# Last layer of a two-layer decoder: the product of attention weights and values taken for two sequences in one matmul, its two PSUM banks split by halves of the heads, and normalised once for every two units

## The chip, the core and the metric

The kernel runs on one core of one Trainium2 chip. The metric is device time in microseconds (us) of one execution. Five engines run their own instruction streams and meet only through semaphores: TensorE (PE, with its weight loads shown apart as PEld), VectorE (DVE), ScalarE (ACT), GpSimd (POOL) and SyncE (SP, which here only issues DMAs).

## The reference, cut to what matters

The program is a decoder of two layers over 32 sequences of 64 tokens with 256 channels. The change lies in the second layer's attention, a differential attention with 16 heads, each with two sub-heads of 8 channels (queries q1, q2 and keys k1, k2) and 16 channels of values that both sub-heads share. `attn1` and `attn2` are causal softmax attention of the two sub-heads over the same 16 value channels.

```python
attn1 = causal_attn_pair(q1, k1, v1, v2, mask, scale)   # softmax(q1 k1^T) [v1 v2]
attn2 = causal_attn_pair(q2, k2, v1, v2, mask, scale)
lambda_full = lambda_1 - lambda_2 + LAMBDA_INIT
f1, f2 = rfft(attn1, axis=1), rfft(attn2, axis=1)       # over the 64 tokens
attn_freq = (f1 - lambda_full * f2) * filt
attn = irfft(attn_freq, n=tgt_len, axis=1)
attn = attn * rsqrt(mean(attn * attn, -1) + EPS) * rms_weight * (1 - LAMBDA_INIT)
return attn.reshape(bsz, tgt_len, H * 2 * D) @ Wout
```

After it the layer adds a summary of a context, normalises, and multiplies by a ternary weight matrix. All of that runs in the same stage as the attention, for other blocks.

## The kernel before, in words

The last layer (`layer1` in the code) works on 8 blocks of 256 tokens (4 sequences). In a block, c = 0, 1 counts chunks of 128 tokens, which are two sequences (s = 0, 1) of 64 tokens side by side on the 128 partitions. A block has 8 units u: chunk c = u // 4, half of the heads m = u // 2 % 2, and quarter hf = u % 2. A unit holds 8 sub-heads, that is 4 heads.

What a unit goes through, each engine one or more slots after the other:

- POOL `keys` spreads the keys over a block-diagonal tile (`k_bd`, L1860).
- PE `score` multiplies queries with `k_bd` and adds the mask (L1973, L1975).
- DVE `row_max` takes the row maximum (L2277) and its negative (L2278).
- ACT `exps` takes 8 exponentials with their row sums `rs` (L2094).
- PE `turn_exp` transposes the exponentials (L1983), and DVE (even units, L2284) or ACT (odd units, L2152) copies them into `et`. `et` has the two sub-heads times the 64 keys of a sequence on its partitions, and for each head 128 columns: the 64 query tokens of sequence 0, then those of sequence 1.
- PE `pv` multiplies `et` with the values `v_bd` (L2000). `v_bd` is block diagonal over the two sub-heads, 32 columns for each head and sequence. For every head there are two matmuls, one for each sequence: 64 columns of `et` as weights, 32 columns of values streamed, written to the 64 rows of that sequence in bank `p_o[c]`. One bank thus holds all 32 sub-heads of a chunk.

After the four units of a chunk, DVE `scale(b, c)` takes the reciprocal of the 32 row sums (L2289), multiplies those of the second sub-heads by minus lambda (L2290), multiplies the bank by them (L2293) and adds the two sub-heads (L2298) into `d`. PE `mix` then applies the filter over the tokens as a matrix (L2009), ACT and DVE take the RMS norm (`rms`, L2138, L2304 to L2311, the power -1/2 on POOL at L1868, `rms_end` at L2315 and L2318), PE transposes (L1940) and multiplies by Wout (L2023), and DVE `wout` adds the residual (L2323).

The order is written out by hand. Every engine runs `for t in range(-1, NBLK + 3)` and in it slots `u in range(8)`. In slot u of pass t the unit is g = 8t + u. PE issues in a slot: `turn_exp(g-1)`, `pv(g-3)`, `score(g+2)`, and then the extras of the slot (u=0 `wout(t-2)` and `t1(t+1)`, u=1 `val(t+1)`, u=2 to 5 `qk(t+1, u-2)`, u=3 `mix(t-1)`, u=4 and 5 the last matmuls of block t-3, u=7 `attn_t(t-1)`). DVE issues `copy_exp(g-2)` for even g, then `wout(t-2)` in slot 1, then `scale(t-1, 1)` in slot 3 and `scale(t, 0)` in slot 7 (behind `rms_end(t-1)`), then `row_max(g+1)`, then `rope_qk(t+1, u-3)` in slots 3 to 6 (two products L2251, four sums L2268), then statistics, `x_apply` and others. Each engine keeps this order strictly: an instruction that waits holds all behind it.

ACT `val` writes `v_bd` for the next block but one (L2130), after the last `pv` that read the same buffer.

Of the kernel before, what the change touches and what calls it, by code (L numbers as in the profile page):

```python
# [9 lines left out]
BATCH, SEQ, DIM = 32, 64, 256  # L10
P = 128
# [3 lines left out]
TC = TOK // P  # L15
# [30 lines left out]
H1, D1 = 16, 8  # L46
SUB = 2 * H1
USUB = 8
NUNIT = SUB // USUB * TC
# [29 lines left out]
def wait(eng, sem, count):  # L79

    if isinstance(count, int) and count <= 0:
        return
    eng.wait_ge(sem, count)


def memory(nc, st):
# [6 lines left out]
    def place(at, *tensors):  # L93

        for name, shape, *dt in tensors:
# [61 lines left out]
                ("rope", [P, 2, TOK]), ("zn", [P, TC, DIM]), ("hi_q", [P, TC, DIM]), ("xa", [P, TC, DIM]),  # L157
                ("xq", [P, TC, DIM], bf16), ("xq_t", [P, KC, TOK], bf16), ("k_bd", [P, 2, USUB, SEQ]),
                ("ex", [P, 2, USUB, SEQ]), ("et", [P, 2, 4 * P]), ("k_st", [P, 2, 4, TC, SEQ]),
                ("yg", [P, 2, TC, DIM]), ("v_bd", [P, 2, TC, 2, H1, 32]),  # L160
                ("osc", [P, TC, SUB * 16]), ("d", [P, TC, DIM]), ("sq", [P, TC * DIM]))
    assert end <= Q0
    end = place(N0, ("sum_w0", [P, KC, DIM]), ("sum_w1", [P, KC, DIM]), ("wq_a", [P, KC, DIM]),
# [1528 lines left out]
def layer1(nc, T, sem, A, E, ctx_sum, ctx_total, summary, x_sh, yt, w_in, b_in, w_out, b_out, w_qk, w_v,  # L1692
# [5 lines left out]
    ALU, ACT, AX = mybir.AluOpType, mybir.ActivationFunctionType, mybir.AxisListType  # L1698
# [26 lines left out]
    S = {n: sem("z_" + n) for n in names}  # L1725
# [20 lines left out]
    def blocks(*b):  # L1746
        return all(0 <= n < NBLK for n in b)
# [181 lines left out]
    def tensor(pe):  # L1929
# [58 lines left out]
        def pv(g):  # L1988
            b, u = g // NUNIT, g % NUNIT
            c, m, hf = UT[u]  # L1990
            pe.wait_ge(S[f"e_read{g % 2}"], g // 2 + 1)
            if u == 0:
                pe.wait_ge(S["a_read"], PA["val", b] + 1)
            if u % 4 == 0:
                wait(pe, S["os_ready"], 2 * (b - 1) + c + 1)
            for q in range(4):
                h = 4 * (2 * m + hf) + q
                for s in range(2):
                    rows = slice(SEQ * s, SEQ * s + SEQ)
                    mm = nc.tensor.matmul(p_o[c][rows, h * 32:h * 32 + 32],  # L2000
                                          et[:, g % 2, q * P + SEQ * s:q * P + SEQ * s + SEQ],
                                          v_bd[:, b % 2, c, s, h, :], start=True, stop=True)
            mm.then_inc(S["pv_done"], 1)

        def mix(b):
            pe.wait_ge(S["d_ready"], 2 * (b + 1))
            done = tenant("b", "circ", b)
            for c in range(TC):
                mm = nc.tensor.matmul(p_b[:, c * DIM:c * DIM + DIM], circ[:, :], d[:, c, :],  # L2009
                                      start=True, stop=True)  # L2010
            mm.then_inc(done, 1)
# [72 lines left out]
    def scalar(act):  # L2084
        def exps(g):
            b, u = g // NUNIT, g % NUNIT
            c, m, hf = UT[u]
            act.wait_ge(S["mx_ready"], g + 1)
            wait(act, S["e_done"], g - 1)
            if u % 4 == 0:  # L2090
                wait(act, S["os_ready"], 2 * (b - 2) + c + 1)
            for j in range(USUB):
                at = USUB * (2 * m + hf) + j
                ins = nc.scalar.activation(ex[:, g % 2, j, :], p_s[g % 2][:, j * SEQ:j * SEQ + SEQ], ACT.Exp,  # L2094
                                           bias=nmx[:, g % 2, j:j + 1], scale=SCALE1,
                                           accum_out=rs[:, b % 2, c, at:at + 1])
            ins.then_inc(S["p_exp"], 1)

        def apply(n, b, src, dst, ready):
            act.wait_ge(RSTD[n][0], RSTD[n][1] + b + 1)  # L2100
            for c in range(TC):
                ins = nc.scalar.activation(dst[:, c, :], src[:, c, :], ACT.Identity,
                                           bias=nbias[:, n, c:c + 1], scale=nrs[:, n, c:c + 1])
            ins.then_inc(S[ready], 1)

        def norm1(b):
            wait(act, S["a_done"], PA["t1", b - 1] + 1 if b else 0)
            apply(1, b, x3[:, b % NX3], n1, "n1_ready")

        def norm_z(b):  # L2110
            wait(act, S["y_sum"], b)
            apply(2, b, x4[:, b % 2], zn, "z_norm")

        def norm_y(b):
            apply(3, b, zn, zn, "y_norm")

        def t1(b):
            act.wait_ge(S["a_done"], PA["t1", b] + 1)
            nc.scalar.activation(xt1[:, :, :].rearrange("p a b -> p (a b)"), p_a[:, :], ACT.Copy
                                 ).then_inc(S["a_read"], 1)  # L2120

        def val(b):

            act.wait_ge(S["a_done"], PA["val", b] + 1)
            wait(act, S["pv_done"], NUNIT * (b - 1))
            act.wait_ge(A["s_set"], A_SET + 4)
            pm = p_a[:, :].rearrange("p (c h e) -> p c h e", c=TC, e=16)
            for s in range(2):
                for o in range(2):
                    ins = nc.scalar.activation(  # L2130
                        v_bd[SEQ * o:SEQ * o + SEQ, b % 2, :, s, :, 16 * o:16 * o + 16],
                        pm[SEQ * s:SEQ * s + SEQ, :, :, :], ACT.Copy)
            ins.then_inc(S["a_read"], 1)

        def rms(b):
            act.wait_ge(S["b_done"], PB["circ", b] + 1)
            wait(act, S["ss_ready"], b)
            nc.scalar.activation(sq[:, :], p_b[:, :], ACT.Abs, scale=RMS_SCALE).then_inc(S["abs_done"], 1)  # L2138
            wait(act, S["b_done"], PB["at", b - 1] + 1 if b else 0)
            nc.scalar.activation(att[:, :, :].rearrange("p a b -> p (a b)"), p_b[:, :], ACT.Copy  # L2140
                                 ).then_inc(S["b_read"], 1)

        def at_copy(b):
            act.wait_ge(S["b_done"], PB["at", b] + 1)
            wait(act, S["b_done"], PB["wout", b - 1] + 1 if b else 0)
            nc.scalar.activation(att_t[:, :, :].rearrange("p a b -> p (a b)"), p_b[:, :], ACT.Copy
                                 ).then_inc(S["b_read"], 1)

        def copy_exp(g):
            act.wait_ge(S["e_done"], g + 1)  # L2150
            wait(act, S["pv_done"], g - 1)
            nc.scalar.activation(et[:, g % 2, :], p_e[g % 2][:, :], ACT.Copy).then_inc(S["e_read1"], 1)  # L2152

        for t in range(-1, NBLK + 3):
            for u in range(NUNIT):
                g = NUNIT * t + u
                if units(g):
                    exps(g)
                if units(g - 2) and g % 2:
                    copy_exp(g - 2)  # L2160
                if u == 0 and blocks(t - 2):
                    at_copy(t - 2)
                if u == 0 and blocks(t + 1):
                    norm1(t + 1)
                if u == 1 and blocks(t + 1):
                    t1(t + 1)
                if u == 2 and blocks(t + 1):
                    val(t + 1)
                if u == 3 and blocks(t - 2):
                    norm_z(t - 2)  # L2170
                if u == 4 and blocks(t - 1):
                    rms(t - 1)
                if u == 6 and blocks(t - 2):
                    norm_y(t - 2)
# [44 lines left out]
    def vector(dve):  # L2219
# [63 lines left out]
            wait(dve, S["pv_done"], g - 1)  # L2283
            nc.vector.tensor_copy(et[:, g % 2, :], p_e[g % 2][:, :]).then_inc(S["e_read0"], 1)  # L2284

        def scale(b, c):

            dve.wait_ge(S["pv_done"], NUNIT * b + 4 * c + 4)
            ch(nc.vector.reciprocal(rin[:, c, :], rs[:, b % 2, c, :]))  # L2289
            ch(nc.vector.tensor_scalar(rin[:, c, 1:SUB:2], rin[:, c, 1:SUB:2], neg_lam[:, 0:1], None,  # L2290
                                       ALU.mult))
            o4 = osc[:, c, :].rearrange("p (h e) -> p h e", e=16)
            nc.vector.tensor_tensor(o4, p_o[c][:, :].rearrange("p (h e) -> p h e", e=16),  # L2293
                                    rin[:, c, :].unsqueeze(2).broadcast_to([P, SUB, 16]), ALU.mult
                                    ).then_inc(S["os_ready"], 1)
            dve.wait_ge(S["os_ready"], 2 * b + c + 1)
            wait(dve, S["b_done"], PB["circ", b - 1] + 1 if b else 0)
            nc.vector.tensor_tensor(d[:, c, :].rearrange("p (h e) -> p h e", e=16),  # L2298
                                    o4[:, 0:SUB:2, :], o4[:, 1:SUB:2, :], ALU.add
                                    ).then_inc(S["d_ready"], 1)  # L2300

        def rms(b):
# [65 lines left out]
        for t in range(-1, NBLK + 3):  # L2368
            for u in range(NUNIT):
# [2 lines left out]
                    copy_exp(g - 2)  # L2372
                if u == 1 and blocks(t - 2):
                    wout(t - 2)
                if u == 3 and blocks(t - 1):
                    scale(t - 1, 1)
                if u == 7 and blocks(t - 1):
                    rms_end(t - 1)
                if u == 7 and blocks(t):
                    scale(t, 0)  # L2380
                if units(g + 1):
                    row_max(g + 1)
                if 3 <= u < 7 and blocks(t + 1):
# [175 lines left out]
```

## Time and profile before

| | us |
|---|---|
| median of 3 runs | 1423.94 (1422.11 to 1428.29) |
| profiled execution, its own time | 1428.95 |
| span of the trace | 1427.1 |
| DVE busy over the span | 937.0 (66%) |
| PE busy over the span | 1127.2 (79%) |
| first and last `pv` matmul (L2000) start | 1055.8 and 1377.0 |

The stage of the last layer is the last 400 us or so of the span. In the rows further down, times count from the start of the span. In a timeline a row is: start us, duration us, engine, line, operation, output<-input with partitions x elements of one instruction, xcount of neighbours merged into the row, and in brackets the idle time of the engine just before it and what ended it. In a list by line it is: line, engine, operation, output<-input, shapes, xcount | busy us, mean ns of one | idle before and what ended it. A row of one source line has the shortest, median and longest duration in ns.

### The profile page before, as it was taken

To read this page: it belongs to the slowest core of one execution; us is meant where nothing else is said; L and a number is where in the kernel's file an instruction comes from. 1 tells how busy PE (TensorE), PEld (TensorE's weight loads), DVE (VectorE), ACT (ScalarE), POOL (GpSimd) and SP (SyncE) were. 2 spreads that over 40 slices of the span, in tenths; PEclk is the share of its full clock that TensorE was granted. 3 is DMA by queue.
4 is the path that set the end of the run, shared out by engine and by line. 5 is a ranking of instruction groups with operands and counts; after the bars stand their busy time and mean duration, and the time that the engine had idled before them with its cause. 6 is when DMAs were issued, how large, how long until landed. Compare 5 with 4: busy or idle time off the path is not lost. (4 is left out here: it accounts for less than half of the span.)

```text
span 1427.1 us, 25403 instructions
## 1 busy us (share of the span) xinstructions
PE 1127.2 (79%) x8276; PEld 968.5 (68%) x8338; DVE 937.0 (66%) x2266; ACT 564.7 (40%) x1990; POOL 536.6 (38%) x575
## 2 busy tenths in 40 slices
PE   6999897987879797954695799998488777787653
PEld 6889886887878686954584679986355555565431
DVE  5656876685867677676772447654167777978753
ACT  5434342432323242312242223332166665676541
POOL 1112122243324142233232346666223355554554
PEclk9999999999989999975897999999599988998875
DMA  5320100101010101014464767765200001000000
GB/s 169 118 68 15 35 5 24 35 14 57 13 50 17 46 20 32 28 33 150 140 183 126 174 127 118 117 107 84 73 16 8 23 9 30 16 9 16 9 22 23
DMA packets 72663, 84.13 MB, mean 59 GB/s; under 512 B 11720, under 2 KB 62632, under 8 KB 72408
## 3 DMA queue, kind: packets, MB, share of 16 engines
q1 hardware_dynamic: 55608, 60.74, 14.3%
q0 software_dynamic: 14592, 19.41, 8.1%
q10 hardware_dynamic: 2336, 2.36, 0.5%
q8 instruction: 71, 1.16, 0.3%
q14 instruction: 56, 0.46, 0.1%
HBM read 49.90 MB, written 32.58 MB: 58 GB/s over the span
## 5 line engine op out<-in xcount | busy, mean ns | idle before, releaser
L740 ACT ACTIVATE qk<-bank,b_col 128x256 f32<-128x256 f32 x256 | 107.3, 472 | 267.6 <-PE bank L516 265.0
L2094 ACT ACTIVATE ex<-bank,nmx 128x64 f32<-128x64 f32 x512 | 153.4, 337 | 88.6 <-DVE nmx L2278 81.8
L414 POOL TENSOR_TENSOR probs<-shifted,rowinv 64x512 f32<-64x512 f32 x64 | 71.0, 1109 | 271.3 <-DVE rowinv L911 201.1
L514 PE MATMUL bank<-xt_hi,w_hi 128*128 128x256 f32 x512 | 155.9, 304 | 5.3 <-DVE w_lo L875 4.9
L515 PE MATMUL bank<-xt_lo,w_hi 128*128 128x256 f32 x512 | 149.7, 292 | 0.0
L516 PE MATMUL bank<-xt_hi,w_lo 128*128 128x256 f32 x512 | 149.2, 291 | 0.0
L1860 POOL TENSOR_TENSOR k_bd<-k_st,bd_mask 128x512 f32<-128x512 f32 x64 | 67.9, 1063 | 173.7 <-PE bank L1975 152.2
L2094 ACT ACTIVATION_READ_ACCUMULATOR ex<-bank,nmx 128x1 f32 x512 | 117.4, 229 | 0.0
L514 PEld LDWEIGHTS bank<-xt_hi,w_hi 128*128 128x128 f32 x512 | 103.6, 202 | 6.4 <-issue 4.5
L756 ACT ACTIVATE at_hi<-bank,b_col 128x256 fp32r<-128x256 f32 x128 | 53.8, 472 | 128.2 <-PE bank L575 128.2
L1547 ACT ACTIVATE act_e<-bank 128x176 f32<-128x176 f32 x112 | 35.5, 317 | 174.4 <-PE bank L1442 174.4
L515 PEld LDWEIGHTS bank<-xt_lo,w_hi 128*128 128x128 f32 x512 | 103.7, 203 | 0.0
L516 PEld LDWEIGHTS bank<-xt_hi,w_lo 128*128 128x128 f32 x512 | 103.1, 201 | 0.0
L514 PE MATMUL bank<-wo_hi,at_hi 128*128 128x256 f32 x256 | 76.3, 298 | 19.4 <-DVE at_lo L923 17.7
L1596 DVE SCALAR_TENSOR_TENSOR act_e<-act_e,bank 128x176 f32<-128x176 f32 x112 | 37.7, 336 | 81.3 <-ACT act_e L1547 80.0
L1496 PE MATMUL bank<-down,act_t 88*128 x320 | 86.4, 393 | 1.9 <-DVE y_sb L1613 1.9
L1680 POOL DMA_INDIRECT x_sh<-y_sb,xe x40 | 62.4, 1560 | 64.7 <-DVE y_sb L1613 54.4
L575 PE MATMUL bank<-pt,v 128*128 128x128 f32 x512 | 74.1, 290 | 14.6 <-DVE pt L917 14.6
L1975 PE MATMUL bank<-k_bd,q_bd 128*128 128x512 f32 x128 | 73.3, 657 | 11.9 <-ACT ex L2094 7.9
L1962 PE MATMUL bank<-xt,qk_w 128*128 128x256 f32 x256 | 68.7, 415 | 15.7 <-ACT v_bd L2130 12.0
L575 PEld LDWEIGHTS bank<-pt,v 128*128 128x128 f32 x512 | 66.0, 201 | 17.3 <-DVE pt L917 16.2
L466 POOL DMA_INDIRECT xs<-xg,slot x64 | 69.9, 1093 | 20.1 <-POOL xg L463 20.1
(298 smaller groups left out, 3234.6 us busy)
## 6 DMA issues: line engine op xcount, KB each, us to landing
xe<-xs SPq DMA_DIRECT2D x80, 136.0 KB, 2.7
e_stage<-w_up SPq DMA_DIRECT2D x18, 352.0 KB
terms<-w_qkv SPq DMA_DIRECT2D x12, 512.0 KB, 5.2
down<-w_down SPq DMA_DIRECT2D x16, 176.0 KB
xs<-zero SPq DMA_DIRECT2D x17, 136.0 KB, 1.9
yt<-zero ACTq DMA_DIRECT2D x1, 2176.0 KB, 8.3
xin<-x SPq DMA_DIRECT2D x8, 256.0 KB, 3.1
terms<-w_o SPq DMA_DIRECT2D x4, 512.0 KB, 4.6
```

The costliest lines, as they stand in the source:

```text
L414: pool.tensor_tensor(probs[r, :, SEQ * s:SEQ * s + SEQ], expd[r, :, :], rowinv[r, :].unsqueeze(2).broadcast_to([SEQ, TC * GH, SEQ]), ALU.m ...
L466: pool.indirect_dma_start(out=xs, out_offset=bass.IndirectOffsetOnAxis(ap=slot[:, TC * b + c, k:k + 1], axis=0), in_=xg[:, b % 2, c, :], i ...
L514: nc.tensor.matmul(out, l_hi, r_hi, start=start, stop=False, skip_group_check=True)
L515: nc.tensor.matmul(out, l_hi, r_lo, start=False, stop=False, skip_group_check=True)
L516: return nc.tensor.matmul(out, l_lo, r_hi, start=False, stop=stop, skip_group_check=True)
L575: mm = nc.tensor.matmul(p_pv[:, e, c * P:c * P + P], v[:, par, c, hh * D0:hh * D0 + D0], pt[:, a, e * TC + c, :], start=True, stop=True)
L740: ins = nc.scalar.activation(qk[:, par, hh, o, :], p_proj[hh % 2][:, o * TOK:o * TOK + TOK], ACT.Identity, bias=b_col[:, o, h:h + 1])
L1496: mm = nc.tensor.matmul(p_y[:, 0:DIM], act_t[:, s % 2, h * P:h * P + P], w[:, h, :], start=first and h == 0, stop=last and h == 1)
L1860: pool.tensor_tensor(k_bd[:, g % 2, :, :], k_st[:, b % 2, 2 * m + hf, c, :].unsqueeze(1).broadcast_to([P, USUB, SEQ]), bd_mask[:, :].unsqu ...
L1962: mm = nc.tensor.matmul(p_a[:, o * TOK:o * TOK + TOK], qk_w[:, 2 * which + o, k, m * P:m * P + P], xt1[:, k, :], start=k == 0, stop=k == K ...
L1975: nc.tensor.matmul(p[:, :], q_bd[:, b % 2, 2 * m + hf, c, :], k_bd[:, g % 2, :, :].rearrange("p a b -> p (a b)"), start=False, stop=True, ...
L2094: ins = nc.scalar.activation(ex[:, g % 2, j, :], p_s[g % 2][:, j * SEQ:j * SEQ + SEQ], ACT.Exp, bias=nmx[:, g % 2, j:j + 1], scale=SCALE1, ...
```

## The change

The matmul of `pv` now takes all 128 columns of `et` of a head as weights and streams 64 columns of values, 32 for each sequence. It fills 128 rows by 64 columns, of which the rows of a sequence use only the 32 columns of that sequence. There are 4 matmuls in a unit where there were 8. A bank now holds half of the heads of a chunk, so the bank is chosen by m and not by c: units 2m and 2m+1 of a chunk fill `p_o[m]`, and it is normalised after every two units: `scale(b, c, m)`, four times in a block, in DVE's slots 1, 3, 5 and 7. The product with the reciprocals is split in two instructions of 64 partitions, one for each sequence, since each picks other columns. `v_bd` changes its layout so that both sequences of a head are neighbours.

```diff
-("yg", [P, 2, TC, DIM]), ("v_bd", [P, 2, TC, 2, H1, 32]),
+("yg", [P, 2, TC, DIM]), ("v_bd", [P, 2, TC, H1, 2, 32]),
@@ tensor: pv
-            if u % 4 == 0:
-                wait(pe, S["os_ready"], 2 * (b - 1) + c + 1)
+            if hf == 0:
+                wait(pe, S["os_ready"], 4 * b + 2 * c + m - 1)
             for q in range(4):
                 h = 4 * (2 * m + hf) + q
-                for s in range(2):
-                    rows = slice(SEQ * s, SEQ * s + SEQ)
-                    mm = nc.tensor.matmul(p_o[c][rows, h * 32:h * 32 + 32],
-                                          et[:, g % 2, q * P + SEQ * s:q * P + SEQ * s + SEQ],
-                                          v_bd[:, b % 2, c, s, h, :], start=True, stop=True)
+                at = (4 * hf + q) * 64
+                mm = nc.tensor.matmul(p_o[m][:, at:at + 64], et[:, g % 2, q * P:q * P + P],
+                                      v_bd[:, b % 2, c, h, :, :].rearrange("p s e -> p (s e)"),
+                                      start=True, stop=True)
             mm.then_inc(S["pv_done"], 1)
@@ tensor: mix
-            pe.wait_ge(S["d_ready"], 2 * (b + 1))
+            pe.wait_ge(S["d_ready"], 4 * (b + 1))
@@ scalar: exps
             if u % 4 == 0:
-                wait(act, S["os_ready"], 2 * (b - 2) + c + 1)
+                wait(act, S["os_ready"], 4 * (b - 2) + 2 * c + 2)
@@ scalar: val
-                        v_bd[SEQ * o:SEQ * o + SEQ, b % 2, :, s, :, 16 * o:16 * o + 16],
+                        v_bd[SEQ * o:SEQ * o + SEQ, b % 2, :, :, s, 16 * o:16 * o + 16],
@@ vector: scale
-        def scale(b, c):
...
+        def scale(b, c, m):
+
+            half = 4 * b + 2 * c + m
+            dve.wait_ge(S["pv_done"], NUNIT * b + 4 * c + 2 * m + 2)
+            at = slice(16 * m, 16 * m + 16)
+            ch(nc.vector.reciprocal(rin[:, c, at], rs[:, b % 2, c, at]))
+            ch(nc.vector.tensor_scalar(rin[:, c, 16 * m + 1:16 * m + 16:2], rin[:, c, 16 * m + 1:16 * m + 16:2],
+                                       neg_lam[:, 0:1], None, ALU.mult))
+            o4 = osc[:, c, 256 * m:256 * m + 256].rearrange("p (h j e) -> p h j e", j=2, e=16)
+            pv = p_o[m][:, :].rearrange("p (h s j e) -> p h s j e", s=2, j=2, e=16)
+            for s in range(2):
+                rows = slice(SEQ * s, SEQ * s + SEQ)
+                ins = nc.vector.tensor_tensor(
+                    o4[rows], pv[rows, :, s, :, :],
+                    rin[rows, c, at].rearrange("p (h j) -> p h j", j=2).unsqueeze(3)
+                    .broadcast_to([SEQ, 8, 2, 16]), ALU.mult)
+                if s == 0:
+                    ch.also(ins)
+            ins.then_inc(S["os_ready"], 1)
+            dve.wait_ge(S["os_ready"], half + 1)
             wait(dve, S["b_done"], PB["circ", b - 1] + 1 if b else 0)
-            nc.vector.tensor_tensor(d[:, c, :].rearrange("p (h e) -> p h e", e=16),
-                                    o4[:, 0:SUB:2, :], o4[:, 1:SUB:2, :], ALU.add
+            nc.vector.tensor_tensor(d[:, c, P * m:P * m + P].rearrange("p (h e) -> p h e", e=16),
+                                    o4[:, :, 0, :], o4[:, :, 1, :], ALU.add
                                     ).then_inc(S["d_ready"], 1)
@@ vector: the order of a pass
                 if u == 1 and blocks(t - 2):
                     wout(t - 2)
+                if u == 1 and blocks(t - 1):
+                    scale(t - 1, 1, 0)
                 if u == 3 and blocks(t - 1):
-                    scale(t - 1, 1)
+                    scale(t - 1, 1, 1)
+                if u == 5 and blocks(t):
+                    scale(t, 0, 0)
                 if u == 7 and blocks(t - 1):
                     rms_end(t - 1)
                 if u == 7 and blocks(t):
-                    scale(t, 0)
+                    scale(t, 0, 1)
                 if units(g + 1):
                     row_max(g + 1)
```

## Rows read from the trace of the kernel before

**Rows 1.** Busy time over the span and in one block's window.

```profile
PE 1127.2 (79%) x8276; PEld 968.5 (68%) x8338; DVE 937.0 (66%) x2266; ACT 564.7 (40%) x1990; POOL 536.6 (38%) x575
...
1209.00:1253.00 44.00, 34.67 (x257) 25.53 (x260) 36.15 (x89) 28.91 (x146) 23.12 (x23) 0.88 0.06 19
```

**Rows 2.** Timeline of DVE, blocks of pass 3 to 6: their additions behind Wout.

```profile
1164.45 0.69 DVE L2323 TENSOR_TENSOR x<-x,bank 128x512 f32<-128x512 f32 x1 [5.77 <-PE bank L2023]
...
1209.65 0.69 DVE L2323 TENSOR_TENSOR x<-x,bank 128x512 f32<-128x512 f32 x1 [4.95 <-PE bank L2023]
...
1298.19 0.69 DVE L2323 TENSOR_TENSOR x<-x,bank 128x512 f32<-128x512 f32 x1 [5.16 <-PE bank L2023]
```

**Rows 3.** Timeline of DVE, the block that starts at 1209.65.

```profile
1224.39 0.76 DVE L2251 TENSOR_TENSOR rope<-bank,rope_t 128x256 f32<-128x256 f32 x2 [0.18 <-PE bank L1962]
...
1229.47 0.68 DVE L2277 TENSOR_REDUCE rmx<-bank 128x8 f32<-128x512 f32 x1
...
1236.14 0.76 DVE L2251 TENSOR_TENSOR rope<-bank,rope_t 128x256 f32<-128x256 f32 x2 [0.64 <-PE bank L1962]
1236.93 3.44 DVE L2268 TENSOR_TENSOR k_st<-rope 64x128 f32<-64x128 f32 x4
...
1243.33 0.34 DVE L2289 RECIPROCAL rin<-rs 128x32 f32<-128x32 f32 x1
1243.71 0.24 DVE L2290 TENSOR_SCALAR rin<-rin,neg_lam 128x16 f32<-128x16 f32 x1
1243.99 0.69 DVE L2293 TENSOR_TENSOR osc<-bank,rin 128x512 f32<-128x512 f32 x1
1244.71 0.49 DVE L2298 TENSOR_TENSOR d<-osc 128x256 f32<-128x256 f32 x1
1245.12 0.68 DVE L2277 TENSOR_REDUCE rmx<-bank 128x8 f32<-128x512 f32 x1
```

**Rows 4.** DVE by line over the span, and the duration spread of some lines.

```profile
L911 DVE RECIPROCAL rowinv<-rowsum 128x8 f32<-128x8 f32 x32 | 6.5, 203 | 1.1
L2290 DVE TENSOR_SCALAR rin<-rin,neg_lam 128x16 f32<-128x16 f32 x16 | 6.2, 388 | 0.6
...
L2293 DVE TENSOR_TENSOR osc<-bank,rin x16: 691/691/692, 1071.2 to 1381.1; 128x512 f32<-128x512 f32 x16
L2298 DVE TENSOR_TENSOR d<-osc x16: 424/456/1311, 1071.9 to 1381.8; 128x256 f32<-128x256 f32 x16
L2268 DVE TENSOR_TENSOR k_st<-rope x64: 282/287/1328, 1030.8 to 1330.2; 64x128 f32<-64x128 f32 x64
L2278 DVE TENSOR_SCALAR nmx<-rmx x64: 170/172/1231, 1041.5 to 1363.3; 128x8 f32<-128x8 f32 x64
```

**Rows 5.** Timeline of DVE in the passes with less work, and the last.

```profile
1063.31 0.76 DVE L2251 TENSOR_TENSOR rope<-bank,rope_t 128x256 f32<-128x256 f32 x2 [0.55 <-PE bank L1962]
...
1079.01 0.69 DVE L2277 TENSOR_REDUCE rmx<-bank 128x8 f32<-128x512 f32 x1 [3.59 <-PE bank L1975]
...
1130.27 0.76 DVE L2251 TENSOR_TENSOR rope<-bank,rope_t 128x256 f32<-128x256 f32 x2 [1.12 <-PE bank L1962]
...
1365.24 0.19 DVE L2315 TENSOR_TENSOR ssr<-ssr,keep 128x32 f32<-128x32 f32 x1 [1.20 <-POOL ssr L1868]
```

**Rows 6.** Chain of waits: a `pv` unit. Timeline of PE: eight 128-wide loads.

```profile
1210.49 0.59 PE bank L2000 x16
...
703.53 0.96 PE L636 MATMUL bank<-gate_w,xgt 128*128 128x16 f32 x8
704.34 0.41 PE L1440 MATMUL bank<-sh_hi,et_hi 128*128 128x352 f32 x1
```

**Rows 7.** POOL beside the long `k_st` row of DVE.

```profile
1237.49 1.39 POOL L1877 TENSOR_TENSOR zn<-zn,gamma_r 128x512 f32<-128x512 f32 x1 [0.21 <-ACT zn L2102]
```

**Rows 8.** The chain that ended last, at the end of the stage.

```profile
1381.85 0.43 DVE d L2298
...
1382.33 2.09 PE bank L2009 x4
```

More of the change, by code:

```diff
@@ L2284, in copy_exp @@
             nc.vector.tensor_copy(et[:, g % 2, :], p_e[g % 2][:, :]).then_inc(S["e_read0"], 1)
-        def scale(b, c):
[L2288 to L2296, printed above, removed]
+        def scale(b, c, m):
[17 more added lines that the diff above has]
+            dve.wait_ge(S["os_ready"], half + 1)
             wait(dve, S["b_done"], PB["circ", b - 1] + 1 if b else 0)
-            nc.vector.tensor_tensor(d[:, c, :].rearrange("p (h e) -> p h e", e=16),
-                                    o4[:, 0:SUB:2, :], o4[:, 1:SUB:2, :], ALU.add
+            nc.vector.tensor_tensor(d[:, c, P * m:P * m + P].rearrange("p (h e) -> p h e", e=16),
+                                    o4[:, :, 0, :], o4[:, :, 1, :], ALU.add
                                     ).then_inc(S["d_ready"], 1)
```

## The prediction

> **What bounds the kernel now.** I read the busy shares first. PE leads over the span with 79%, but in a window of one block of the last layer DVE is the busier of the two: 36.15 us of 44 against 34.67 [rows 1]. A share doesn't say which engine paces, so the timeline of DVE through one block came next. The reader is to look at the brackets there, the idle time ahead of a row. The addition behind Wout at 1209.65 had waited 4.95 us for PE. From there to 1245.12 the brackets add up to 0.18 + 0.64 = 0.82 us of waiting in 35.5 us [rows 2, 3]: DVE runs its list with hardly a hole, and the work of slots 1 to 7 goes at DVE's pace. Four passes look so, with the same addition from 1164.45 to 1298.19; the four addition starts (1164.45, 1209.65, one between them and the last, 1298.19) are 133.74 / 3 = 44.6 us apart [rows 2]. In them time on DVE behind that addition is time on the path. The wait of 5 us lies ahead of the addition and can cover nothing that the change puts behind it. The chain that ended last agrees at the stage's end: the addition of `d`, then at once the filter on PE [rows 8].
>
> **The change on DVE.** A whole `scale` takes 1245.12 - 1243.33 = 1.79 us of DVE's list: 0.38 from reciprocal to lambda product, 0.28 to the large product, 0.72 to the sum, 0.41 to the next instruction [rows 3]. A half consists of:
> - a reciprocal of 16 sums. 8 take 203 ns, 32 take 340 [rows 4, 3]: 0.25, with the hand-over of 0.04 that the whole one shows, 0.29;
> - the lambda product of 8 elements: 0.17 to 0.24 [rows 3, 4], taken as 0.20, with hand-over 0.24;
> - two products from PSUM of 64 partitions by 256 elements. A row as long is the pair of L2251, 256 elements from PSUM each, one behind the other: 0.76 [rows 3], with hand-over 0.79. Half the partitions save nothing; the whole one had 512 elements in one instruction for 0.69;
> - a sum of 128 elements, as the shortest of L2268: 0.28 [rows 4].
>
> Together 1.60 us. Low end 1.45 (the smaller values, no hand-overs); high end 2.2 (the four-level pattern costs each product as much as the whole one's 0.69, [rows 4]). So four halves cost 6.4 us in a block where two wholes cost 3.6: halving saves next to nothing of the time of one `scale`, and there are twice as many.
>
> The Trainium skill speaks against the change in the same way: "VectorE: DVE Perf Modes", section on the TRN2 errata, says that instructions with an SBUF source pay a fixed extra time each and that small tiles pay it again and again. By an estimate from that page's fixed term of about 150 cycles at 0.96 GHz (0.156 us), six more instructions per chunk are 0.94 us, and the 512 elements more per partition 0.53: 1.79 + 1.47 = 3.26 for two halves, against my 3.20.
>
> **Where these fall.** Slots 3 and 7 hold a half instead of a whole: -0.19 each. Slots 1 and 5 get a half that was not there, each ahead of a `row_max`: +1.60. In slot 5 (ahead of 1229.47) no DVE wait stands in the way; the later wait of 0.64 is for PE matmuls that themselves follow a DVE copy of the same slot, so it moves along and covers nothing. In slot 1 (behind the addition at 1209.65) the list runs full well into slot 4, where the first wait, at 1224.39, is 0.18 [rows 2, 3]. Behind the inserted instructions stand `row_max` and through it ACT's exponentials, then PE. A full pass: 1.60 - 0.18 - 0.19 + 1.60 - 0.19 = 2.64 us, four of them 10.6.
>
> The other passes have other covers [rows 5]:
> - pass 0, slot 5 only: 0.18 and 0.55 us of waiting for PE absorb; 1.60 - 0.73 - 0.19 = 0.7.
> - pass 1: slot 1 comes in a wait of 3.59 for the score; the score matmuls stand right behind the awaited `pv`, so most of the half is hidden, 0.3 left; slot 5 is full, 1.4: 1.7.
> - pass 2: slot 1 is mostly taken up by a wait of 1.12 later: 0.4; slot 5 1.4: 1.8.
> - pass 7: slots 1 and 3 lead to `d` and the filter, 1.4; slot 5 meets a wait of 1.20 for POOL, of which I count half, 0.9: 2.3.
> - pass 8: slots 1 and 3 lead to the filter that the last chain shows waiting for `d` [rows 8]: 1.4.
>
> Sum: 0.7 + 1.7 + 1.8 + 10.6 + 2.3 + 1.4 = 18.5 us.
>
> **Collisions with GpSimd.** The same DVE instruction takes 0.28 or up to 1.33 us (`k_st`), 0.17 or 1.23 (`nmx`), 0.42 or 1.31 (`d`) [rows 4]. The row of four `k_st` at 1236.93 takes 3.44 instead of about 1.24 while POOL runs products such as the one of 1.39 us that starts 0.56 us later [rows 3, 7]. The large product out of PSUM never shows it: 691 to 692 ns in all 16. "GPSIMD Engine Reference" of the Trainium skill, section Specifications, names the cause: GpSimd shares its SBUF interfaces with VectorE, and VectorE instructions in a two-port mode or with two SBUF inputs contend. The trace agrees line by line. So the added lambda products and sums are exposed, the added large products not. Sixteen lambda products lost (388 - 240) ns each on average; the sums about as much. That would be 0.3 us for each added half if nothing else moved, 0.6 a block; since a POOL instruction that hits an added one may spare the next, the ends are 0 and 1.3 (one POOL instruction more per block). I take 0.6 in six blocks: 3.6 us.
>
> **The change on PE.** A unit's 16 records now take 0.59 us [rows 6]. Two passes of 4 matmuls make 8 records, but with 128-wide loads. The nearest row has 8 such loads with streams of only 16 columns: 704.34 - 703.53 = 0.81 [rows 6]. So `pv` would take 0.8 to 0.86, 0.25 more and not less, though the instructions halve: 64 x 0.25 = 16 us of PE time. On the path in slots 1 to 3 lie two or three of them, 0.5 to 0.75 us, while DVE is 1.4 late there: covered. I count 0; ends -0.3 a unit (loads free, streams as short as the row's) and all 16 us. The new wait of `pv` is for the half two earlier. That half is done in DVE slots 1, 3, 5, 7, the waiting `pv` comes in PE's slots 3, 5, 7, 1 behind: two slots of room where there were four, some 10 us. Behind a late one would stand `score`; I count 0. The layout of `v_bd` changes only ACT's strides: 0.
>
> **The sum.** 18.5 + 3.6 = 22 us on the profiled execution's 1428.95 gives 1451. That execution lies 5 us above the median of the runs, 1423.94; on the median it is 1446, which is my forecast, +1.5%. Its own range: some 28 halves lie on the path (four in each of passes 3 to 7, two in each of the other four). At 1.45 us and without collisions they give 18.5 - 28 x 0.15 = 14, or 1438; at 1.9 us with them 22 + 28 x 0.3 = 30, or 1454. The high end of 2.2 us would make it 39, or 1463.
>
> **The rivals.**
> - *PE takes the pace in slots 1 to 3.* For it: PE is at 34.67 of 44 us in the window, and 0.25 us more come in every unit. Against: DVE is delayed more than PE at each meeting point. Price: the whole 16 us on top, 1462. It decides where PE's delay exceeds DVE's 1.4.
> - *The half in slot 1 is hidden.* For it: early passes show waits behind it. Against: 0.18 us in the full ones. The slot 1 terms go, 4 x 1.42 + 0.3 + 0.4 + 1.4 + 1.4 = 9: 1437.
> - *Faster: the shift of DVE against POOL clears collisions.* In one block DVE loses 3.44 - 1.24 = 2.2 us in `k_st` [rows 3] and, where each is hit once, 1.06 in `nmx` and 0.9 in `d` [rows 4], about 4.2. POOL's power of -1/2 starts before the half in slot 5 and not behind it, so POOL's products move about 1 us against `k_st`. If all went in six blocks: 18.5 - 25 = -6.5, 1417. It decides above 2.64 us a block, more than half of all collisions. Against: POOL's products hang on DVE's statistics and mostly move along, and a shift of 1 us against three products in a row hits as likely more.
> - *No change*: DVE's list isn't the path at all. Against it the 0.82 us of waits.
>
> **How the numbers follow.** Forecast 0.68, PE's pace 0.11, slot 1 hidden 0.10, no change 0.06, faster 0.05. A measurement can tell about 0.5% (7 us) from no change; the first three cases are slower by more. The range reaches down to the hidden slot 1 and up over the forecast's own 1454 a part of the way to 1462 and 1463: 1436 to 1459. It leaves out no change, faster and most of PE's pace, 0.2 together.
>
> **What would show it.** In the trace after: DVE's time from the addition behind Wout to slot 7's `row_max` grows from 35.5 to about 38.5 us, the wait ahead of the addition stays near 5 us, passes are 47 to 48 us apart instead of 44.6, a half takes 1.6 us, a `pv` unit 0.8 to 0.86. The forecast is wrong if a half takes under 1.2 us, if DVE gets new waits for PE of over 1 us in slots 1 to 6, or if the `k_st` row of slot 6 drops to 1.24.

## The result, and the profile after

The changed kernel takes 1453.95 us (median of 4 runs, 1451.97 to 1455.57) against 1423.03 (4 runs, 1419.36 to 1428.29) for the kernel before. The ratio is 1.023, 95% interval 1.019 to 1.027, so 26 to 38 us more. The profiled execution took 1453.49 us, 24.5 more than that of before (1428.95), with a span of 1451.7. The forecast of 1446 had the sign and the place right and was 8 us short on the median, 2.5 us short on the two profiled executions (22 of 24.5). Those two flatter it: the profiled execution of before is the slowest of its four, so their difference is 24.5 where the medians differ by 31. What is read from the two traces below accounts for the 24.5 only.

The first fence is from the page and its windows: the same lines as [rows 1], one block of the last layer. The windows' columns are start:end, length, busy time and count of PE, PEld, DVE, ACT and POOL, granted clock, DMA share, GB/s.

```profile
PE 1145.7 (79%) x7771; PEld 996.1 (69%) x7826; DVE 963.3 (66%) x2362; ACT 564.9 (39%) x1990; POOL 537.6 (37%) x575
...
1216.00:1265.00 49.00, 37.43 (x192) 28.40 (x194) 38.97 (x101) 28.23 (x145) 22.18 (x22) 0.89 0.06 17
```

DVE and PE gained 26.3 and 18.5 us of busy time. Where it counts is to be seen in DVE's timeline. First the additions behind Wout again, as in [rows 2]:

```profile
1166.10 0.69 DVE L2331 TENSOR_TENSOR x<-x,bank 128x512 f32<-128x512 f32 x1 [5.13 <-PE bank L2022]
...
1216.69 0.69 DVE L2331 TENSOR_TENSOR x<-x,bank 128x512 f32<-128x512 f32 x1 [5.73 <-PE bank L2022]
...
1364.13 0.69 DVE L2331 TENSOR_TENSOR x<-x,bank 128x512 f32<-128x512 f32 x1 [4.74 <-PE bank L2022]
```

Passes 3 to 6 last (1364.13 - 1166.10) / 4 = 49.51 us each. Those of before lasted (1342.99 - 1164.45) / 4 = 44.64. Four passes cost 19.5 of the span's 24.6 us. The rest of the ledger, from the same additions: the stage started 0.9 us earlier; passes up to 1 took 0.7 less, pass 2 3.3 more, pass 7 0.8 more, pass 8 2.6 more, the end the same.

Inside the pass that starts at 1216.69, DVE's timeline has the lines that answer to [rows 3]:

```profile
1217.29 0.24 DVE L2290 RECIPROCAL rin<-rs 128x16 f32<-128x16 f32 x1
1217.57 0.23 DVE L2291 TENSOR_SCALAR rin<-rin,neg_lam 128x8 f32<-128x8 f32 x1
1217.84 0.87 DVE L2297 TENSOR_TENSOR osc<-bank,rin 64x256 f32<-64x256 f32 x2
1218.75 0.29 DVE L2306 TENSOR_TENSOR d<-osc 128x128 f32<-128x128 f32 x1
1219.07 0.69 DVE L2276 TENSOR_REDUCE rmx<-bank 128x8 f32<-128x512 f32 x1
...
1230.18 2.90 DVE L2267 TENSOR_TENSOR q_bd<-rope 64x128 f32<-64x128 f32 x4
...
1250.87 0.76 DVE L2250 TENSOR_TENSOR rope<-bank,rope_t 128x256 f32<-128x256 f32 x2 [3.46 <-PE bank L1962]
1251.66 1.92 DVE L2267 TENSOR_TENSOR k_st<-rope 64x128 f32<-64x128 f32 x4
...
1256.26 0.24 DVE L2290 RECIPROCAL rin<-rs 128x16 f32<-128x16 f32 x1
...
1258.04 0.69 DVE L2276 TENSOR_REDUCE rmx<-bank 128x8 f32<-128x512 f32 x1
```

Three things are to be seen. A half takes 1219.07 - 1217.29 = 1.78 us, and again 1258.04 - 1256.26 = 1.78: as long as a whole one of before. The wait for the fourth projection, ahead of the rope product of slot 6, is 3.46 us where it was 0.64. And a long row of four sums is now `q_bd` (2.90), while the long `k_st` row has become shorter (1.92 instead of 3.44): the collisions with POOL moved.

The wait of 3.46 has its cause in PE's timeline of the same stretch:

```profile
1237.60 1.00 PE L1999 MATMUL bank<-v_bd,et 128*128 128x64 f32 x8
1238.43 0.38 PE L1973 MATMUL bank<-mask,ident 128*128 128x512 bf16 x1
...
1244.82 2.72 PE L2043 MATMUL bank<-ffn_w,xq_t 128*128 128x256 bf16 x12 [5.14 <-DVE xq_t L2364]
1247.33 3.51 PE L1962 MATMUL bank<-xt,qk_w 128*128 128x256 f32 x8
```

and in PE's timeline of the kernel before, for the same place in pass 3 and in pass 4:

```profile
1187.69 2.32 PE L2044 MATMUL bank<-ffn_w,xq_t 128*128 128x256 bf16 x12 [2.13 <-DVE xq_t L2356]
1189.81 2.76 PE L1962 MATMUL bank<-xt,qk_w 128*128 128x256 f32 x8
...
1232.90 1.47 PE L2044 MATMUL bank<-ffn_w,xq_t 128*128 128x256 bf16 x12 [2.13 <-DVE xq_t L2356]
1234.20 1.89 PE L1962 MATMUL bank<-xt,qk_w 128*128 128x256 f32 x8
```

DVE copies `xq_t` behind the new half of slot 5 and behind all that was late already. PE idled 5.14 us for it instead of 2.13, and then ran the same 12 and 8 records in 2.72 and 3.51 us instead of the 1.47 and 1.89 of pass 4 before. The windows say what differs: the granted clock (the figure before the last two) of the stretch with these matmuls is 0.52 in the changed kernel, near the lower level of 1.2 GHz,

```profile
1238.00:1244.70 6.70, 1.67 (x9) 0.82 (x8) 6.21 (x19) 2.39 (x16) 4.93 (x1) 0.93 0.00 0
1244.80:1250.80 6.00, 5.98 (x22) 4.58 (x23) 2.44 (x8) 1.09 (x2) 4.68 (x7) 0.52 0.00 1
```

and 1.00, the full 2.4 GHz, in pass 4 of before:

```profile
1232.90:1235.90 3.00, 3.00 (x20) 2.65 (x21) 2.43 (x8) 0.00 (x0) 2.92 (x3) 1.00 0.02 5
```

In the passes 3 to 6 of before the wait of slot 6 was 2.31, 0.64, 0.64 and 2.21, in sum 5.8; of after 3.15, 3.46, 2.44 and 2.15, in sum 11.2. The wait follows the clock, and not directly the idle time: pass 3 of before, with the same idle 2.13 us ahead, ran its 20 records in 2.32 and 2.76 us (granted clock 0.68 from 1187.69 to 1193.00), 1.7 us more than pass 4, and its wait is 1.7 us longer; in pass 4 of after the records take 2.9 us more than in pass 4 of before, and the wait is 2.8 us longer. The lower clock was thus there before the change in two of the four passes, and in all four after it.

So the 19.5 us of four passes are: halves 4 x (4 x 1.78 - 2 x 1.79) = 14.2; waits for the projections in slots 3 to 6 together 11.2 - 6.8 = 4.4; waits ahead of the additions -0.6; the remainder 1.5, which fits the collisions but was not measured in these passes by itself.

### The profile page after: what moved, and what is told of

The parts are those of the page before. It is cut to its first block and busy times, and to the rows that moved or that the text cites. A ratio compares the mean times of both kernels' runs of the same rounds, so it can differ in the third digit from the quotient of the medians.

```text
span 1451.7 us, 24512 instructions
## 1 busy us (share of the span) xinstructions
PE 1145.7 (79%) x7771; PEld 996.1 (69%) x7826; DVE 963.3 (66%) x2362; ACT 564.9 (39%) x1990; POOL 537.6 (37%) x575
## 5 line engine op out<-in xcount | busy, mean ns | idle before, releaser
L1962 PE MATMUL bank<-xt,qk_w 128*128 128x256 f32 x256 | 73.0, 436 | 17.6 <-ACT v_bd L2129 9.7
L1962 PEld LDWEIGHTS bank<-xt,qk_w 128*128 128x128 f32 x256 | 54.1, 219 | 38.3 <-ACT v_bd L2129 16.0
L923 DVE SCALAR_TENSOR_TENSOR at_lo<-bank,b_col,at_hi 128x256 fp32r<-128x256 f32 x128 | 55.6, 476 | 31.9 <-ACT at_hi L756 31.6
```

Source lines behind the costliest of these rows:

```text
L1962: mm = nc.tensor.matmul(p_a[:, o * TOK:o * TOK + TOK], qk_w[:, 2 * which + o, k, m * P:m * P + P], xt1[:, k, :], start=k == 0, stop=k == K ...
```

## The experiments

Every kernel was timed in 5 rounds beside the kernel before on the same chip; "over before" is the ratio less 1, times 1424 us, with its interval.

**pe_wide: TensorE's side alone.**

```diff
 (before)
-                for s in range(2):
-                    rows = slice(SEQ * s, SEQ * s + SEQ)
-                    mm = nc.tensor.matmul(p_o[c][rows, h * 32:h * 32 + 32], ...
+                h2 = min(h, H1 - 2)
+                mm = nc.tensor.matmul(p_o[c][:, h2 * 32:h2 * 32 + 64], et[:, g % 2, q * P:q * P + P],
+                                      v_bd[:, b % 2, c, 0, h2:h2 + 2, :].rearrange("p a b -> p (a b)"),
+                                      start=True, stop=True)
```

> The kernel before with TensorE's side of the change alone: in pv each head is one matmul of 128 weight columns by 64 streamed columns, 4 in a unit where there were 8, banks and VectorE as before. It leaves out that sequence 1 gets its own values (it multiplies with those of sequence 0) and neighbouring heads overwrite each other. Theory VectorE (its list of instructions sets the pace, TensorE's extra time is covered): a pv unit takes 0.8 to 0.86 us against 0.59, and the kernel 0 to 5 us more than before. Rival TensorE (its extra time is on the path): 64 x 0.25 = 16 us more, or over half of the 31 us that the change costs.

Measured: 1424.24 us, ratio 1.0007 (0.9977 to 1.0037): +1 us (-3 to +5). PE's timeline shows a unit at 0.84 us from start to the next:

```profile
1209.85 1.00 PE L1999 MATMUL bank<-v_bd,et 128*128 128x64 f32 x8
1210.69 0.38 PE L1973 MATMUL bank<-mask,ident 128*128 128x512 bf16 x1
```

and DVE's timeline that it is felt, but only as short waits:

```profile
1215.43 0.76 DVE L2250 TENSOR_TENSOR rope<-bank,rope_t 128x256 f32<-128x256 f32 x2 [0.28 <-PE bank L1962]
...
1220.37 0.76 DVE L2250 TENSOR_TENSOR rope<-bank,rope_t 128x256 f32<-128x256 f32 x2 [1.39 <-PE bank L1962]
```

PE's 16 us more of work (64 units at 0.84 instead of 0.59) cost nothing that could be measured, so the rival in which all of it lies on the path is out. The zero is a balance, though. In passes 3 to 6 DVE waited 3.6 us more in front of the rope products than in the kernel before (10.5 against 6.8), and its busy rows and small gaps took 3.4 us less; why they did was not tested.

**narrow_split: VectorE's side alone.**

```diff
 (changed kernel; in place of its 4 matmuls)
+                for s in range(2):
+                    rows, at = slice(SEQ * s, SEQ * s + SEQ), (4 * hf + q) * 64 + 32 * s
+                    mm = nc.tensor.matmul(p_o[m][rows, at:at + 32],
+                                          et[:, g % 2, q * P + SEQ * s:q * P + SEQ * s + SEQ],
+                                          v_bd[:, b % 2, c, h, s, :], start=True, stop=True)
```

> The changed kernel with the matmuls of before (8 in a unit, 64 weight columns by 32 streamed), its banks by halves, four normalisations of a block and split products kept. Theory VectorE: 24 to 31 us over the kernel before, like the changed kernel. Rival TensorE: under 12 us over it, as the wide loads are gone.

Measured: 1454.13 us, ratio 1.019 (1.015 to 1.023): +27 us (21 to 33), against +32 (26 to 38) for the changed kernel. The change's cost is there without the wide matmuls; what they add to it, if anything, is within the noise.

**narrow_one: the same with a shorter half.**

```diff
 (narrow_split; in pv both sequences now write the columns at = (4 * hf + q) * 32)
-            for s in range(2):
...
+            nc.vector.tensor_tensor(
+                osc[:, c, 256 * m:256 * m + 256].rearrange("p (a e) -> p a e", e=16),
+                p_o[m][:, 0:256].rearrange("p (a e) -> p a e", e=16),
+                rin[:, c, at].unsqueeze(2).broadcast_to([P, 16, 16]), ALU.mult).then_inc(S["os_ready"], 1)
```

> As narrow_split, but each normalisation is one product of 128 partitions by 256 elements, possible since each sequence's rows are written at the same columns. A half should take 0.28 + 0.24 + 0.46 + 0.32 = 1.30 us instead of the changed kernel's 1.78. Theory VectorE: in a full pass 4 x 1.30 - 2 x 1.79 = 1.62 us more than before instead of 3.54, so about half of the change's cost stays: 10 to 16 us over the kernel before. A rival that only the number of normalisations counts (a semaphore step, a fixed wait each): 24 us or more over it, as in narrow_split.

Measured: 1434.90 us, ratio 1.0074 (1.0043 to 1.0105): +11 us (6 to 15), as expected. DVE's timeline shows the half at 1213.01 - 1211.79 = 1.22 us:

```profile
1211.79 0.25 DVE L2291 RECIPROCAL rin<-rs 128x16 f32<-128x16 f32 x1
1212.07 0.23 DVE L2292 TENSOR_SCALAR rin<-rin,neg_lam 128x8 f32<-128x8 f32 x1
1212.34 0.42 DVE L2295 TENSOR_TENSOR osc<-bank,rin 128x256 f32<-128x256 f32 x1
1212.80 0.29 DVE L2301 TENSOR_TENSOR d<-osc 128x128 f32<-128x128 f32 x1
1213.01 0.68 DVE L2277 TENSOR_REDUCE rmx<-bank 128x8 f32<-128x512 f32 x1
```

One product less in each half, 0.56 us by this row, takes off 16 us by the ratios: 32 halves at 0.56 would be 18. The number of normalisations alone doesn't decide; their time on DVE's list does, and with it the waits that lateness causes.

**wide_s1 and wide_s15: covers for the added halves.**

```diff
 (changed kernel; both)
-                if u == 1 and blocks(t - 2):
-                    wout(t - 2)
                 if u == 1 and blocks(t - 1):
                     scale(t - 1, 1, 0)
+                if u == 1 and blocks(t - 2):
+                    wout(t - 2)
 (wide_s15 too; scale(t, 0, 0) taken from ahead of row_max)
                 if u == 5 and blocks(t - 3):
                     xq_copy(t - 3)
+                if u == 5 and blocks(t):
+                    scale(t, 0, 0)
```

> The changed kernel with the half of slot 1 moved ahead of the addition behind Wout, into the 4 to 6 us that VectorE waits there for TensorE. Theory VectorE: the half (1.78 us) leaves the path in passes 2 to 8, 7 x 1.78 = 12 us less than the changed kernel, so 16 to 22 us over the kernel before. Rival (slot 1 was covered anyway): no change, 28 us or more over the kernel before.

> The changed kernel with the half of slot 1 ahead of the addition behind Wout (as wide_s1) and the half of slot 5 behind the copy xq_copy, where VectorE later waits 2.2 to 3.5 us for TensorE. Theory VectorE with covers: both added halves lie beside waits, the halves of slots 3 and 7 cost what the wholes did, so the time is within 5 us of the kernel before, on either side. Rival (VectorE's total work decides wherever it stands): 3.5 us a pass more remain for the shorter waits, 15 us or more over before, as wide_s1.

Measured: wide_s1 1440.24 us, ratio 1.012 (1.009 to 1.016), +18 us (12 to 23): about what the theory said. In its trace the passes 3 to 6 are 46.7 us apart where they were 49.5, so a pass gains more than the half's 1.78; the waits of slot 6 have shrunk too, from 11.2 to 7.3 us in the four, while slots 3 and 4 now show the 7.2 us of waiting for PE that the half had covered. wide_s15 1441.44 us, ratio 1.011 (1.006 to 1.015), +15 us (9 to 22): the second cover gave nothing that can be told. The expectation failed (it was within 5 us of the kernel before), and PE's timeline of wide_s15 agrees with this reason:

```profile
1239.48 1.47 PE L2043 MATMUL bank<-ffn_w,xq_t 128*128 128x256 bf16 x12 [1.95 <-DVE xq_t L2364]
1240.79 1.89 PE L1962 MATMUL bank<-xt,qk_w 128*128 128x256 f32 x8
```

With the copy ahead of the half PE waited 1.95 and not 5.14 us (3.75 in wide_s1), its matmuls took what they take at the full clock in all four passes, and the wait of 2 to 3.5 us in which the half was to hide did not exist any more. DVE's timeline has its fourth rope product without any bracket, and the sums behind it in a collision:

```profile
1244.60 0.74 DVE L2250 TENSOR_TENSOR rope<-bank,rope_t 128x256 f32<-128x256 f32 x2
1245.38 3.91 DVE L2267 TENSOR_TENSOR k_st<-rope 64x128 f32<-64x128 f32 x4
```

A wait that the lateness itself had made was no cover. What was there without it was 0.64 us, as in the passes of before at the full clock.

**wide_xq and wide_s1_xq: the copy that PE waits for, first.**

```diff
 (changed kernel; slot 5 of VectorE; wide_s1_xq with the edit of wide_s1 too)
+                if u == 5 and blocks(t - 3):
+                    xq_copy(t - 3)
                 if u == 5 and blocks(t):
                     scale(t, 0, 0)
...
-                if u == 5 and blocks(t - 3):
-                    xq_copy(t - 3)
```

> The changed kernel with the copy of the quantised block (xq_copy) moved in slot 5 from behind the rope sums to the front, ahead of the half there. TensorE waits for that copy and then does the last matmuls of a block and the fourth projection; in the changed kernel it had idled about 5 us before them and ran them at the lower clock (12 records in 2.72 us, the projection in 3.31; 1.47 and 1.74 in one block of before). Theory clock and wait: TensorE starts on them some 4.6 us earlier, VectorE's wait of 2.2 to 3.5 us ahead of the fourth rope product goes to under 1 us in the passes 3 to 6, and the time falls by 6 to 12 us against the changed kernel, to 18 to 24 over the kernel before. Rival (the halves alone cost it all; the wait is made up later): within 4 us of the changed kernel, 26 or more over before.

> The changed kernel with both moves, the half of slot 1 ahead of the addition behind Wout and xq_copy at the front of slot 5. If the two add up, 31 - 15 - 6 = 10 us over the kernel before, which would be the half of slot 5 alone (1.78 us in seven passes are 12). Rival (they share a cause): 15 us over before, as with the first alone.

Measured: wide_xq 1447.61 us, ratio 1.017 (1.013 to 1.021), +24 us (18 to 30). That is 6 us under the changed kernel by the medians; the intervals of the two ratios overlap, so the size is not sure. PE's timeline shows what was expected of it:

```profile
1234.07 1.47 PE L2043 MATMUL bank<-ffn_w,xq_t 128*128 128x256 bf16 x12 [0.49 <-DVE xq_t L2364]
```

In no pass from 3 to 6 does DVE wait over 0.3 us ahead of the fourth rope product (2.15 to 3.46 in the changed kernel). Part of it was given back one row later: in pass 4 the four `k_st` sums take 4.25 us there (DVE's timeline).

```profile
1241.46 0.75 DVE L2250 TENSOR_TENSOR rope<-bank,rope_t 128x256 f32<-128x256 f32 x2 [0.26 <-issue]
1242.24 4.25 DVE L2267 TENSOR_TENSOR k_st<-rope 64x128 f32<-64x128 f32 x4
```

wide_s1_xq: 1437.38 us, ratio 1.008 (1.006 to 1.011), +12 us (8 to 16). It was expected at 10 if the two moves add up, and the half of slot 5 alone, 1.78 us in seven passes, would be 12. The run does not separate that half from the collisions that moved with the copy.

**before_late, before_xq, before_late_xq, narrow_one_s15: towards a better kernel.**

```diff
 (before; before_late)
+                if u == 1 and blocks(t - 1):
+                    scale(t - 1, 0)
                 if u == 1 and blocks(t - 2):
                     wout(t - 2)
...
-                if u == 7 and blocks(t):
-                    scale(t, 0)
 (before_xq: only xq_copy(t - 3) to the front of slot 5; before_late_xq: both)
```

> The kernel before with its scale(t, 0) moved from slot 7 to slot 1 of the next pass, ahead of the addition behind Wout: the same work, in VectorE's wait of about 5 us for TensorE. Theory VectorE: 1.79 us leave the path in seven passes, 9 to 14 us less than the kernel before. Rival (the wait is filled, but TensorE then waits for VectorE or the clock falls): within 4 us of before.

> The kernel before with xq_copy alone moved to the front of slot 5. Theory clock and wait: 2 to 6 us less than the kernel before, since it has waits of 0.64 to 2.3 us there in passes 3 to 6. Rival: no change within 2 us, the gain is lost to collisions.

> before_late (scale(t, 0) in slot 1 of the next pass, ahead of the addition behind Wout) with xq_copy also moved to the front of slot 5. Theory clock and wait: TensorE's wait of some 2 us for that copy goes, so does VectorE's wait of 0.6 to 2.3 us ahead of the fourth rope product: 3 to 8 us less than before_late, 14 to 18 us under the kernel before. Rival (collisions of the rope sums with GpSimd's products grow as in wide_xq, where the four sums of slot 6 went to 4.25 us): within 3 us of before_late.

> narrow_one (the matmuls of before, banks by halves, one product a half, 1.3 us each) with the halves of slots 1 and 5 moved as in wide_s15. Theory VectorE: slots 3 and 7 now have 1.3 us instead of 1.79, so two times 0.5 us less than before in each of seven passes, and the other two halves covered: 2 to 8 us less than the kernel before. Rival (VectorE's total work decides): 5 us or more over it.

Measured: before_late 1412.05 us, ratio 0.992 (0.988 to 0.996), 12 us under before. The work is the same; only its place is another, and DVE's timeline shows it ahead of the addition, whose wait has gone from about 5 to 3.68 us:

```profile
1228.29 0.34 DVE L2289 RECIPROCAL rin<-rs 128x32 f32<-128x32 f32 x1
...
1229.66 0.42 DVE L2298 TENSOR_TENSOR d<-osc 128x256 f32<-128x256 f32 x1
1233.76 0.69 DVE L2323 TENSOR_TENSOR x<-x,bank 128x512 f32<-128x512 f32 x1 [3.68 <-PE bank L2023]
```

The size agrees with the expectation (9 to 14), but the trace does not show it where it was expected, as 1.79 us in each of seven passes. From the second addition to the sixth, passes 3 to 6, before_late takes (1322.30 - 1145.77) / 4 = 44.13 us each against 44.64: 2 us in four passes. The larger part lies earlier, in DVE's timeline from the first rope product of pass 0 to the first of pass 3: in the kernel before 1174.39 - 1055.44 = 118.95 us,

```profile
1055.44 0.76 DVE L2251 TENSOR_TENSOR rope<-bank,rope_t 128x256 f32<-128x256 f32 x2 [1.80 <-PE bank L1962]
...
1174.39 0.76 DVE L2251 TENSOR_TENSOR rope<-bank,rope_t 128x256 f32<-128x256 f32 x2
```

and in before_late 1155.71 - 1049.03 = 106.68, 12.3 us less.

```profile
1049.03 0.76 DVE L2251 TENSOR_TENSOR rope<-bank,rope_t 128x256 f32<-128x256 f32 x2 [1.79 <-PE bank L1962]
...
1145.77 0.69 DVE L2323 TENSOR_TENSOR x<-x,bank 128x512 f32<-128x512 f32 x1 [0.29 <-PE bank L2023]
...
1155.71 0.75 DVE L2251 TENSOR_TENSOR rope<-bank,rope_t 128x256 f32<-128x256 f32 x2
...
1322.30 0.69 DVE L2323 TENSOR_TENSOR x<-x,bank 128x512 f32<-128x512 f32 x1 [3.88 <-PE bank L2023]
```

(Another 6.4 us between the two profiled executions lie ahead of pass 0's first rope product, before the moved work runs at all, and say nothing of the edit: these two executions differ by 20 us, the medians by 11.) In the full passes part of the rival came true: the wait of slot 6 was 0.64, 2.31, 2.19 and 2.22, long in three of four passes where it had been long in two. Why the early passes gain so much was not tested.

before_xq: 1424.08 us, ratio 0.998 (0.995 to 1.001), -3 us (-7 to +1): no gain that can be told from none. before_late_xq: 1404.05 us, ratio 0.985 (0.982 to 0.989), 21 us under before (16 to 26; 14 to 18 were expected), the fastest kernel of this study and more than the two edits alone give (12 and 3). The traces show where: in passes 3 to 6 the additions are 44.6 us apart before, 44.1 in before_late, 44.0 in before_xq and (1319.54 - 1153.33) / 4 = 41.6 with both. With both, the first three passes gain the same 12.2 us as in before_late, PE's 12 records take 1.47 us in all four full passes, and the wait of slot 6, still 1.8 us a pass in before_late, is gone; DVE's other rows do not grow, while in before_xq they grew by 0.8 us a pass and ate most of that gain. What decides between the two was not tested.

narrow_one_s15: 1423.95 us, ratio 1.0009 (0.9982 to 1.0036): no change (-3 to +5) instead of 2 to 8 us less. Slots 3 and 7 save 2 x 0.57, the half of slot 5 (1.22) has a cover of 0.64; that leaves 0.6 a pass, 4 us, which the interval just excludes. Of the places tried, the best for the halves brings no gain.

## Why the prediction was right

**The bound.** Right. DVE's list paces slots 1 to 7: VectorE's side alone costs +27, TensorE's side alone +1. "Four passes look so" was read too smoothly: in passes 3 and 6 the brackets hold not 0.82 us but 2.5 and 2.4, for the waits of 2.31 and 2.21 in slot 6. Of the signs that the prediction named, the wait ahead of the addition stayed near 5 us (4.35 to 5.73 in passes 3 to 6). The time from the addition to slot 7's `row_max` grew to 1258.04 - 1216.69 = 41.35 us and not 38.5, the passes are 49.5 and not 47 to 48 us apart, and one sign of being wrong did appear: in slot 6 DVE waits 3.46 us where it had waited 0.64.

**The half.** 1.60 us forecast, 1.78 measured, within its bounds of 1.45 to 2.2. The term that was mis-sized is the pair of products: 0.79 with hand-over forecast from the pair of L2251 (two of 0.42 in 0.76), 0.91 measured, as the two of 0.42 take 0.87 together. The two rope products of the nearest row overlap by 0.08, these two do not. The recorded ground, that half the partitions save nothing, held; that the pair overlaps as the nearest row does was the part that did not. With the halves at 1.78, a full pass comes to 3.54 - 0.18 = 3.4 and not 2.64, 2.9 us more in four.

**Where they fall.** Slot 1 had no cover (32 - 18 = 14 us, wide_s1) and slot 5 next to none (12 us, wide_s1_xq), as said. Wrong was the sentence that the wait of slot 6 "moves along and covers nothing": it grew, from 5.8 to 11.2 us in four passes, since the matmuls that it waits for ran at a lowered clock (granted 0.52 in pass 4) in all four passes and no longer in two. This is the step of the sum that failed. For all waits on projections in these passes the sum had -0.7 (four times 0.18 covered) and the trace has +4.4, 5.1 us apart. That the new lateness brings the lower clock is argued from the traces: with PE idle for 3.3 us or more ahead of them, the 12 records took over 1.9 us in 15 of 16 passes (changed kernel, narrow_split, narrow_one, wide_s1), with 2.12 or 2.13 us in 6 of 12 (before, before_late, narrow_one_s15), with 1.96 or less in none of 24 (pe_wide, wide_s15 and the four with the copy first). What else decides it, with 2.13 us above all, stays open.

**Where the sum was lucky.** In the four full passes it had 10.6 and 2.4 for collisions, 13.0 us, where the ledger has 19.5. In the other passes it had 7.9 and 1.2, 9.1 us, where the ledger with its earlier start has 5.1. That the sum came within 2.5 us of the profiled difference is two misses, 6.5 short and 4.0 over, that partly cancel.

**The early and late passes.** 7.9 us forecast for passes 0, 1, 2, 7 and 8; by the ledger 6.0 (-0.7 + 3.3 + 0.8 + 2.6). Single ones were off by up to 3 us: passes 0 and 1 should have cost 2.4 and gave back 0.7, with the wait ahead of pass 2's addition 4.26 us where it had been 6.72. What shortened it I did not test.

**Collisions with GpSimd.** 3.6 us forecast; summed over DVE's lines of this stage, busy time less count times the line's shortest duration rose from 34.6 to 36.7 us, 2.1. Part of it moved from the sums of the keys to those of the queries. In the list by line of after:

```profile
L2267 DVE TENSOR_TENSOR q_bd<-rope 64x128 f32<-64x128 f32 x64 | 25.4, 397 | 2.0
L2267 DVE TENSOR_TENSOR k_st<-rope 64x128 f32<-64x128 f32 x64 | 25.1, 392 | 2.0
L2277 DVE TENSOR_SCALAR nmx<-rmx 128x8 f32<-128x8 f32 x64 | 18.4, 288 | 2.2
```

In the list by line of before the `q_bd` row was undisturbed:

```profile
L2268 DVE TENSOR_TENSOR k_st<-rope 64x128 f32<-64x128 f32 x64 | 28.7, 448 | 2.1
L2278 DVE TENSOR_SCALAR nmx<-rmx 128x8 f32<-128x8 f32 x64 | 19.6, 306 | 2.2
L2268 DVE TENSOR_TENSOR q_bd<-rope 64x128 f32<-64x128 f32 x64 | 18.3, 286 | 2.1
```

So the rival in which collisions clear did not come; more of them moved than were added. The 64 products that read PSUM stayed at 415 to 429 ns. The rule of the Trainium skill ("GPSIMD Engine Reference", Specifications), which names VectorE instructions in a two-port mode or with two SBUF inputs, agrees: these products have one input in PSUM and one in SBUF.

**TensorE.** 0.8 to 0.86 us a unit forecast, 0.83 and 0.84 measured. In the changed kernel it was covered: the half in slot 1 comes ahead of the rope products, and none of those in slots 3 to 5 of passes 3 to 6 waits. The new waits of `pv` never showed.

## What to carry to other kernels

When one engine's list has hardly a hole, an edit is worth about what it adds to or takes from that list; here fewer instructions on another engine brought nothing, and a normalisation split in two costs nearly two. Look for the one long wait on that engine and move work ahead of it: 1.79 us of instructions a pass, moved and not changed, gave 12 us here. But look in the trace where the gain fell. It was 0.5 us a pass in the full passes, since another wait came back, and most of it lay in the first three. Before hiding work in a wait, ask whether the wait would be there without the delay one has caused oneself.

## What the runs showed of the hardware

Two products from PSUM of 64 partitions each, on the two halves of the partitions, took 0.87 us for two of 0.42, one behind the other without overlap, while two of 128 partitions, the rope products of about 0.42 each, took 0.76. The two pairs differ in more than their partitions; no run here varies those alone. Eight loads of 128 weight columns with 64 streamed columns took 0.84 us, hardly more than the 0.81 of the eight with 16 streamed columns [rows 6]: four times the stream made almost no difference, so at this length the stream does not set the pace. And the wait of slot 6 follows TensorE's granted clock: with 5.14 us idle ahead, the 20 matmul records took 2.72 + 3.51 us at 0.52; with 2.13 us idle they took 2.32 + 2.76 at 0.68 in one pass and 1.47 + 1.89 at 1.00 in the next.
